# Expert lists ordered by choice, results stored by list, and two indirect reads for each token

## The reference, cut to what matters

```
x = x + fast_weight_attention(layernorm(x))
x = x + ffn(layernorm(x))                    # first expert stage
x = x + causal_attention(layernorm(x))
x = x + ffn(layernorm(x))                    # second expert stage

# ffn: 8 experts, each token goes to two of them
probs = softmax(xf @ gate_w.T);  top_p, top_i = top_k(probs, 2)
w     = top_p / (sum(top_p) + 1e-9)
rank  = place of the token among the tokens with this expert as this choice (first or second)
keep  = rank < 640
out   = sum over the two choices of  w * keep * (silu(xf @ gate[e].T) * (xf @ up[e].T)) @ down[e].T
```

## Time and profile before

| | |
|---|---|
| median of 3 runs | 1765.23 us (1761.93 to 1765.7) |
| the profiled execution, its own time | 1763.04 us |
| its span, first to last instruction | 1760.8 us |
| mean granted TensorE clock | 0.815 of full speed |
| busy: PE / DVE / ACT / POOL | 1211.1 / 992.7 / 629.3 / 554.7 us |
| chain that ended last, largest shares | POOL sides L978 4%, POOL slots L972 3% |
| first expert stage | 511.2 to 779.4 us of the span |
| second expert stage | 1497.0 us to the end |

### The profile page before, as it was taken

One profiled execution on the slowest core, in us unless ns is written; L12 is line 12 of the kernel. 1 busy time (PEld: TensorE's weight loads), 2 busy tenths in 40 slices (PEclk: granted clock), 3 DMA queues, 4 the chain that ended last, 5 costly groups with the idle time before them and its releaser, 6 DMA issues. The chain is left out here.

```text
span 1760.8 us, 26686 instructions
## 1 busy us (share of the span) xinstructions
PE 1211.1 (69%) x9140; PEld 799.2 (45%) x9214; DVE 992.7 (56%) x2284; ACT 629.3 (36%) x989; POOL 554.7 (32%) x627
## 2 busy tenths in 40 slices
PE   4525977959635059804788998999799997412991
PEld 2313856839525049702244443444344443312991
DVE  6865555655426126434776776777577771631662
ACT  4632221212111023202165665666476666101330
POOL 2434013040026747723013102400240000374772
PEclk9766988969755569955599999999899999555996
DMA  1439611020120133160000001001000100213325
GB/s 45 156 148 386 270 37 60 0 95 0 36 63 29 53 104 99 53 187 6 7 19 7 8 19 33 12 9 43 8 7 8 31 7 13 62 53 94 96 68 161
DMA packets 109057, 114.06 MB, mean 65 GB/s; under 512 B 8720, under 2 KB 90512, under 8 KB 108048
## 3 DMA queue, kind: packets, MB, share of 16 engines
q1 hardware_dynamic: 96608, 91.98, 16.6%
q0 software_dynamic: 9216, 19.02, 3.2%
q10 hardware_dynamic: 3120, 1.57, 0.3%
HBM read 49.34 MB, written 59.02 MB: 62 GB/s over the span
## 5 line engine op out<-in xcount | busy, mean ns | idle before, releaser
L1834 DVE TENSOR_REDUCE att_mx<-att_ps 128x1 f32<-128x512 f32 (+3 forms) x768 | 405.4, 555 | 163.8 <-PE att_ps L1727 123.7
L1608 ACT ACTIVATE att_prob<-att_ps 128x1024 f32<-128x1024 f32 (+3 forms) x384 | 300.1, 812 | 218.9 <-PE att_ps L1739 160.6
L1724 PE MATMUL att_ps<-att_kT,att_q1T 128*128 128x512 bf16 (+3 forms) x712 | 236.6, 345 | 34.2 <-DVE att_mx L1834 18.0
L1736 PE MATMUL att_ps<-att_q2T,att_kT 128*128 128x512 bf16 (+3 forms) x750 | 200.3, 330 | 4.2 <-ACT att_prob L1608 1.8
L1724 PEld LDWEIGHTS att_ps<-att_kT,att_q1T 128*128 128x128 bf16 x768 | 74.4, 98 | 235.6 <-DVE att_mx L1834 182.6
L978 POOL DMA_INDIRECT sides<-moe_ys,moe_back_i x160 | 153.2, 957 | 87.5 <-issue 47.3
L1750 PE MATMUL att_pso<-att_prob,att_v 128*32 128x512 f32 (+3 forms) x1536 | 165.4, 503 | 1.5
L972 POOL DMA_INDIRECT slots<-moe_rows,moe_place_i x128 | 123.1, 961 | 59.7 <-issue 38.4
L1503 POOL CAST att_qm_rows<-att_nm 128x32 bf16<-128x32 f32 x48 | 15.5, 323 | 390.7 <-DVE att_nm L1843 386.5
L1727 PE MATMUL att_ps<-att_mask,att_identb 128*128 128x128 bf16 x512 | 115.5, 228 | 2.3 <-DVE att_mx L1834 1.5
L1071 PE MATMUL moe_ps_t<-moe_ident,moe_xs 128*128 128x128 f32 x160 | 27.0, 289 | 115.1 <-DMA moe_xs<-slots 115.1
(11 more groups left out here) (283 smaller groups left out, 2447.7 us busy)
## 6 DMA issues: line engine op xcount, KB each, us to landing
slots<-fw_zeros SPq DMA_DIRECT2D x2, 5200.0 KB, 30.6
moe_xs<-slots SPq DMA_DIRECT2D x16, 650.0 KB, 4.5
sides<-fw_zeros SPq DMA_DIRECT2D x2, 4096.0 KB, 35.2
moe_side<-sides SPq DMA_DIRECT2D x16, 512.0 KB, 6.3
tok<-prep_tok SPq DMA_DIRECT2D x4, 1536.0 KB, 5.4
turned<-prep_tT SPq DMA_DIRECT2D x4, 1536.0 KB, 8.8
fw_tok<-tok SPq DMA_DIRECT2D x4, 1536.0 KB, 10.8
fw_Tkv<-turned SPq DMA_DIRECT2D x4, 1024.0 KB, 7.1
```

Of the source, the lines that this page charges most:

```text
L1608: nc.scalar.activation(prob[(2 * n + pair) % 4][:, :, 0:size], ps2[pair][:, :, 0:size], ACT.Exp, scale=SCORE_SCALE).then_inc(exp_done, 1)
L1724: last = nc.tensor.matmul(out[:, 0:size], q1T[t % 2][:, j * P:(j + 1) * P], kT[t][h][:, 512 * c:512 * c + size], start=True, stop=not diag ...
L1736: last = nc.tensor.matmul(ps2[pair][:, h, 0:size], kT[t][2 * pair + h][:, i * P:(i + 1) * P], q2T[t % 2][:, first:first + size], start=Tru ...
L1834: nc.vector.reduce_max(mx[:, c, j, h:h + 1], ps1[(n * QUAD + h) % 2][:, 0:size], AX.X).then_inc(max_done, 1)
```

## The change

- The lists are ordered by choice: eight first-choice lists, then eight second-choice lists (`base` has other strides). POOL scatters all first choices, then all second choices, and each choice has its own semaphore. SP loads one list (five tiles) at a time into a ring of six buffers, the first eight lists after the first choice's semaphore.
- A list is done in two blocks, of three and two tiles: 32 blocks in a stage.
- Rows are 128 wide: token number and share no longer travel. The shares stay on the chip in `share`.
- A block's result is copied by ACT (`copy_y`) into `ys`, and SP stores it in list order into `results[k]`, one tensor for each choice. `returns`, `weigh` and the 80 scatters to `sides` are gone.
- `places` also makes `fetch_i`, the row of each token in `results[k]`; a token that was not kept reads row 5120, which is cleared.
- POOL reads the rows back with 32 indirect DMAs for each choice, once that choice's eight lists are stored. VectorE adds share x row to x, tile by tile, first choice then second.
- The clears are now the list part of `slots` and 128 rows of each `results` tensor.
- The split of the weights moves to POOL, behind its last work in `fast_weight_stage`, as 16 copies and 16 subtractions.
- `statistics(0)` comes before the waits for setup, `normalize(0)` before `statistics(1)`, and only PE's `ranks` waits for ACT's cast (`tri_cast`).

```diff
-                size = 8 * region.shape[1]
+                size = min(ZEROS, spread.shape[1])
...
+            pool.wait_ge(expert["loaded"], 3 * 16)
+            for whole, (hi, lo) in expert["split"]:
+                for e in range(EXPERTS):
+                    nc.gpsimd.tensor_copy(hi[:, e], whole[:, e])
+                pool.drain()
+                for e in range(EXPERTS):
+                    nc.gpsimd.tensor_tensor(lo[:, e], whole[:, e], hi[:, e].bitcast(F32), ALU.subtract)
...
+BLOCKS = ((0, 3), (3, LIST_TILES))
+ZEROS = 8 * D
...
-    BLOCKS = [(0, 4), (4, 8), (8, EXPERT_TILES)]
     PER = len(BLOCKS)
-    blocks = EXPERTS * PER
-    PARTS = 4
+    blocks = LISTS * PER
+    RING = 6
+    Y_RING = 4
     ctx = ExitStack()
...
-                sp.wait_ge(y_written[s], 16 * sum(BLOCKS[n % PER][1] - BLOCKS[n % PER][0] for n in range(s, blocks, 4)))
+                sp.dma_start(xb[:, b * tiles:(b + 1) * tiles], by_quarter(x_in)[b]).then_inc(x_loaded[b], 16)
+
+            def load(i):
+                if i % EXPERTS == 0:
+                    sp.wait_ge(slots_written[i // EXPERTS], TILE_COUNT * 16)
+                if i >= RING:
+                    sp.wait_ge(t_psum, (i - RING + 1) * PER)
+                sp.dma_start(xs[i % RING][:], slots[i * CAPACITY:(i + 1) * CAPACITY].rearrange("(j p) n -> p j n", p=P)).then_inc(xs_loaded[i % RING], 16)
+
+            for i in range(RING):
+                load(i)
+            for i in range(LISTS):
+                for n, (first, end) in enumerate(BLOCKS):
+                    sp.wait_ge(y_done, i * PER + n + 1)
+                    rows_of = i % EXPERTS * CAPACITY
+                    sp.dma_start(results[i // EXPERTS][rows_of + first * P:rows_of + end * P].rearrange("(j p) d -> p j d", p=P), ys[i % Y_RING][:, first:end]).then_inc(y_stored[i % Y_RING], 16)
+                if i + RING < LISTS:
+                    load(i + RING)
+
             for b in range(quarters):
...
+                sp.wait_ge(summed, b + 1)
+                sp.dma_start(by_quarter(x_out)[b], xb[:, b * tiles:(b + 1) * tiles]).then_inc(stored, 16)
...
-            pool.iota(base_i[:], [[CAPACITY, 2], [2 * CAPACITY, EXPERTS]], base=-1, channel_multiplier=0).then_inc(iotas, 1)
+            pool.iota(base_i[:], [[EXPERTS * CAPACITY, 2], [CAPACITY, EXPERTS]], base=-1, channel_multiplier=0).then_inc(iotas, 1)
...
+            for b in range(quarters):
+                rsqrt(b)
...
+            for k in range(2):
+                for b in range(quarters):
+                    if k == 0:
+                        pool.wait_ge(placed, b + 1)
+                    for j in range(tiles):
+                        pool.indirect_dma_start(slots, bass.IndirectOffsetOnAxis(ap=place_i[b][:, j, k:k + 1], axis=0), rows[:, b * tiles + j], None).then_inc(slots_written[k], 16)
+
+            for k in range(2):
+                for s in range(Y_RING):
+                    pool.wait_ge(y_stored[s], (k + 1) * (EXPERTS // Y_RING) * PER * 16)
+                for b in range(quarters):
+                    for j in range(tiles):
+                        pool.indirect_dma_start(fetched[k][:, b * tiles + j], None, results[k], bass.IndirectOffsetOnAxis(ap=fetch_i[b][:, j, k:k + 1], axis=0)).then_inc(fetches[k][b], 16)
...
+            def copy_y(n):
+                i, (first, end) = n // PER, BLOCKS[n % PER]
+                act.wait_ge(y_psum, n + 1)
+                if i >= Y_RING and first == 0:
+                    act.wait_ge(y_stored[i % Y_RING], i // Y_RING * PER * 16)
+                nc.scalar.activation(ys[i % Y_RING][:, first:end], ps_y[n % 2][:, 0:end - first], ACT.Copy).then_inc(y_done, 1)
...
                         pe.wait_ge(xt_done, 2 * (b - 1) + h + 1)
                     for j in range(4):
-                        last = nc.tensor.transpose(ps_t[h][:, j * P:(j + 1) * P], rows[:, b * tiles + 4 * h + j, 2:2 + D], ident[:])
...
-                nc.vector.tensor_tensor(rows[:, token, D + 3], top[:, 0], wsum[:], ALU.mult)
-                nc.vector.tensor_tensor(rows[:, token, 0], top[:, 1], wsum[:], ALU.mult)
+                for k in range(2):
+                    nc.vector.tensor_tensor(share[:, token, k], top[:, k], wsum[:], ALU.mult)
...
+                for k in range(2):
+                    nc.vector.scalar_tensor_tensor(fetch[:, :, k], place[:, :, k], float(-(k + 1) * EXPERTS * CAPACITY), kept[:, :, k], ALU.add, ALU.mult)
+                dve.drain()
                 nc.vector.tensor_tensor(place[:], place[:], spare_slot[:, token], ALU.subtract)
                 dve.drain()
+                nc.vector.tensor_scalar(fetch_i[b][:], fetch[:], float(EXPERTS * CAPACITY), None, ALU.add)
                 nc.vector.tensor_tensor(place[:], place[:], kept[:], ALU.mult)
                 dve.drain()
...
-            dve.wait_ge(iotas, 3 + EXPERTS)
-            nc.vector.tensor_copy(rows[:, :, 1], ids[:])
-            nc.vector.tensor_copy(rows[:, :, D + 2], ids[:])
+            statistics(0)
+            dve.wait_ge(iotas, 2)
             nc.vector.tensor_copy(spare_slot[:], spare_slot_i[:])
-            nc.vector.tensor_copy(spare_token[:], spare_token_i[:])
             nc.vector.tensor_copy(base[:], base_i[:])
-            dve.wait_ge(weights_in, 4 * 16)
             dve.wait_ge(setup, SETUP)
-            statistics(0)
+            normalize(0)
             statistics(1)
-            normalize(0)
             statistics(2)
             statistics(3)
+            dve.wait_ge(weights_in, 4 * 16)
             for b in range(quarters):
...
+            for k in range(2):
+                for b in range(quarters):
+                    dve.wait_ge(fetches[k][b], tiles * 16)
+                    if k:
+                        dve.drain()
+                    for t in range(b * tiles, (b + 1) * tiles):
+                        last = nc.vector.scalar_tensor_tensor(xb[:, t], fetched[k][:, t], share[:, t, k:k + 1], xb[:, t], ALU.mult, ALU.add)
+                    if k:
+                        last.then_inc(summed, 1)
+
...
-    slots = [scratch(f"slots{n}", [SLOTS + 2 * TOKENS, ROW]) for n in range(2)]
-    sides = [scratch(f"sides{n}", [2 * TOKENS + SLOTS, D]) for n in range(2)]
+    slots = [scratch(f"slots{n}", [SLOTS + 2 * TOKENS, D]) for n in range(2)]
+    results = [[scratch(f"results{n}{k}", [SLOTS // 2 + P, D]) for k in range(2)] for n in range(2)]
```

More of the change, by code:

```diff
@@ L958, in _ @@
-            rsqrt(0)
-            rsqrt(1)
-            if split_weights:
-                for e in range(4, EXPERTS):
-                    split(e)
-            rsqrt(2)
-            rsqrt(3)
-            pool.wait_ge(weights["cleared"], len(weights["to_clear"]) * 16)
-            for b in range(quarters):
-                pool.wait_ge(placed, b + 1)
-                for j in range(tiles):
-                    for k in range(2):
-                        source = rows[:, b * tiles + j, 2:2 + ROW] if k == 0 else rows[:, b * tiles + j, 0:ROW]
-                        pool.indirect_dma_start(slots, bass.IndirectOffsetOnAxis(ap=place_i[b][:, j, k:k + 1], axis=0), source, None).then_inc(slots_written, 16)
@@ L974, in _ @@
-            for n in range(blocks):
-                e, (first, end) = n // PER, BLOCKS[n % PER]
-                pool.wait_ge(y_done, n + 1)
-                for j in range(first, end):
-                    pool.indirect_dma_start(sides, bass.IndirectOffsetOnAxis(ap=back_i[e % 2][:, j:j + 1], axis=0), ys[n % 4][:, j - first], None).then_inc(y_written[n % 4], 16)
+            for b in range(quarters):
+                rsqrt(b)
+            pool.wait_ge(weights["cleared"], len(weights["to_clear"]) * 16)
@@ L1004, in hi @@
             def hi(n):
-                size = P * (BLOCKS[n % PER][1] - BLOCKS[n % PER][0])
+                first, end = BLOCKS[n % PER]
+                size = P * (end - first)
                 act.wait_ge(t_psum, n + 1)
@@ L1020, in _ @@
                         hi(n + 1)
+                if n >= 1:
+                    copy_y(n - 1)
+            copy_y(blocks - 1)
         @block.tensor
@@ L1045, in ranks @@
                 pe.wait_ge(chosen_done, b + 1)
+                pe.wait_ge(tri_cast, 1)
                 if b >= 2:
@@ L1089, in down @@
             def down(n):
-                e, (first, end) = n // PER, BLOCKS[n % PER]
+                e, (first, end) = n // PER % EXPERTS, BLOCKS[n % PER]
                 pe.wait_ge(hid_done, 2 * n + 2)
@@ L1255, in _ @@
-            returns(0)
             lo(0)
             for n in range(blocks):
-                e, size = n // PER, P * (BLOCKS[n % PER][1] - BLOCKS[n % PER][0])
+                first, end = BLOCKS[n % PER]
+                size = P * (end - first)
                 for k in range(2):
```

141 lines of the change are left out of this document (33 added, 108 removed).

## The result

The changed kernel takes 1715.3 us (median of 4 runs, 1714.33 to 1716.7) beside 1765.34 us of the kernel before on the same chip: ratio 0.972, 95% interval 0.970 to 0.974, 50 us faster. Its profiled execution took 1716.7 us. This number has to be read with the experiments: they ran on other chips, and on one of these the same changed kernel was slower than the one before.

What follows compares the result with a forecast made beforehand. Bound: expert stages' serial parts, 80 us of scatters with TensorE idle, 104.4 of matmuls, 39.1 after. Gains of 24.5 (second stage) and 28.9 (first) sum to 53.4: 1765.2 - 53.4 = 1712 us, range 1698 to 1742.

Steps and rivals of the forecast that it cites:

- Way in: Expert stages' start: first choices scattered first, so TensorE starts after 32 scatters, 37.9 us earlier in the second stage.
- index work: Router on VectorE: fetch indices, two small operations, a drain and a cast, add 0.4 us a quarter.
- handoff to TensorE: From the last first-choice scatter's start to TensorE's start: 6.95 us as before, nothing credited for the half-sized load.
- Matmuls: Expert matmul run: eight more blocks at 0.13 us fixed cost each add 1.0 us, 105.5 in place of 104.4.
- rival of waiting TensorE: Expert matmuls: short blocks leave TensorE waiting, each 0.5 us a list costing 8 us a stage, 1728; chance 0.09.
- Price of a fetch: Way out: an indirect read costs the scatter's 1.263 us step, bounds 0.96 and 2.33; dearer below break-even 0.08, near or above 0.06.
- The port: Way out: 56 VectorE sums a stage hold off POOL's last fetches, 15.9 us a stage, 1744 in all; chance 0.05.
- The sum: Both expert stages: gains of 24.5 us (second) and 28.9 us (first) make 53.4, giving 1712 us.
- The fast-weight part: Fast-weight stage: changes only at its edges; the moved weight split, 23.2 us, is free within POOL's 47.08 us idle.
- the 2 us that I had named as a sign of being wrong: Fast-weight or attention stage: a change of more than 2 us in either would show the prediction wrong.
- My case that the work is hidden: First-choice fetches, 40.4 us, run under the matmuls with 11 us to spare; the split, 23.2 us, in POOL's idle time.
- the 110 that I had named as a sign of being wrong: Expert stages: a run of matmuls exceeding 110 us, against 105 expected, would show the prediction wrong.

Runs made afterwards that it cites:

- kernel paced by four: Changed kernel, POOL waiting after every fourth second-choice scatter and first-choice fetch until the four landed; 1740.73 us, ratio 0.954 to the kernel before.
- the two edits: Changed kernel with the first list loaded only after both choices' scatters, 1882.71 us; or with first-choice fetches waiting for all sixteen lists' rows, 1865.1 us.

## Why the prediction was right, point by point

On the chip of the result the forecast of 1712 us met 1715.3, in its own range of 1702 to 1722, and the mechanism was the one described.

- *Way in.* Predicted from the stage's start: last first-choice scatter 75.5, TensorE 82.4 us. Measured 75.95 and 81.2. Quarter 2 is placed at 56.55, not 55.5, because x is there 5.0 us after its issue, not 4.1, and the logits are taken at 19.2 us (1492.19), not 18.1. The index work cost what was estimated: from the logits to quarter 2's places it takes 37.4 us against 36.2 before, 0.4 a quarter. POOL started 0.5 us behind a place, not 1.0, and the handoff to TensorE, for whose half-sized load I gave nothing, took 5.25 us, not 6.95.
- *Matmuls.* 105.5 predicted, 105.3 and 105.1 measured. The rival of waiting TensorE did not happen.
- *Price of a fetch.* This was the largest unknown, taken from the scatter at 1.263 us; it measured 1.249, with 2.6 us to landing, not 2.3. Being nearest by engine, index count and row size, the scatter's row was the right one.
- *The port.* The mis-sized term. I gave it 0.05 as all or nothing, 15.9 us a stage if every sum held POOL off. It is true in part: one fetch in each stage is held, 3.9 us, since 32 of the 56 sums then run back to back; the bursts of eight cost 0.1. My evidence against it were router operations with drains between them. The row with a drain behind the 32nd sum shows a held fetch getting through there, so such a sequence need not show the hold. The Trainium skill, "SBUF — State Buffer", section "Who interferes with whom", says that a VectorE instruction with two SBUF inputs contends with a GpSimd instruction that reads SBUF, and that page adds as inferred, of tensor_tensor, that descriptor generation is spared. The traces agree with the first: the fetch is held to the end of the burst, 13.3 us with a burst twice as long. The second does not carry over to this form of DMA, which reads its row numbers from SBUF; whether that reading or the writing of descriptors is what waits, and that it is the port at all, no run here tells.
- *The sum.* Each stage came out 2.6 and 2.5 us longer than the 239.3 predicted: 3.9 for the held fetch, 0.6 for landing and end, less 1.2 for the start and about 0.7 for steps and matmuls. The fast-weight part, which I took as unchanged, is 2.2 us longer, just past the 2 us that I had named as a sign of being wrong. 1.4 of it stand after 103 us already, in code that is the same, and POOL's moved split begins only at 465.86. The other traces of kernels with this code start the first expert stage at 511.9 to 514.8 us, so one execution can't say that the split costs anything. By the spans the miss is 2.6 + 2.5 + 2.2 + 0.2 = 7.5 us of 53.4; that the medians miss by only 3.3 is luck, since the profiled execution of before lay under its median and that of after over it.
- *What it did not cover.* My case that the work is hidden supposes that POOL's stream leaves the other engines alone. Nothing in the trace of before speaks against it on that chip, and the forecast stands for chips like it. On a held chip the same program is 1.5% slower than before, outside the range in ratio, its matmul run of 178 us is past the 110 that I had named as a sign of being wrong, and none of my rivals is that case.

What stays open: why the chips differ. The held chips show the same median duration of one 384-column matmul, of a scatter and of a fetch (0.34, 0.96 and 0.94 us), so it is the arrival of updates and not the work; whether the chip, its place in the machine or something beside it makes the difference, no run here tells. The traces differ in one more thing: for the same program that of the held chip has 10,331 records of semaphore updates and that of the result 13,667, and the missing ones lie in the expert stages. The kernel paced by four lacks as many (10,574) and yet hardly waits. So the recording may differ on these chips too, and whether the profiler's own writing has a part in the late updates was not tested. What hiding the two streams is worth on the chip of the result, about 40 us each by arithmetic, was not measured there, because the two edits ran on held chips; on its own chip the change is known by the rows of the stages alone.

## What to carry to other kernels

Price an indirect read like the indirect write of the same shape, and look at what else POOL would meet: a long run of two-input VectorE sums without a drain held its next indirect DMA until the run ended, so spread such sums over the time before. Before counting on matmuls beside a stream of indirect DMAs, run the kernel on more than one chip: a stream was free on one here and cost nearly its own length on another. Groups of four with a wait for landing gave 1741 us on a chip of either sort (two variants of it), a ratio to before of 0.954 on the held one and 0.986 on the other, against 1.015 (on another held chip) and 0.970 without; which to choose depends on where the kernel will run.

## What the runs showed of the hardware that was not expected

- Late semaphore updates: up to 34 us between the end of a matmul and the ACT instruction that waits for it alone, inside a stream of indirect DMAs at steps of 1.25 us. Late updates show on three of the chips; none on the chip of the result nor on that of the last sitting. With pauses of 1.5 to 2 us every 5 us the run was 111 us, with pauses every 10 us 152 and 162, against 174 to 178 without on the other two held chips.
- On such a chip VectorE's chain of small operations with drains slowed from 0.30 to 1.40 us a step, some 20 us into a stream of scatters, until the stream paused.
- A held indirect DMA ended 0.8 us after VectorE's run of sums, whatever the hold (4.9, 6.8 and 13.3 us). Those that started up to 1.27 us into a run took 1.13 us at most.
